# From wo on: seven tiles of 128 tokens in place of eight batches of 112, and two new orders of work

## The chip, the cores and the metric

The kernel runs on one core of a Trainium2 chip. The metric is device time in microseconds (us) of one execution, the median of several runs. Engines: TensorE (PE; its weight loads are PEld), VectorE (DVE), ScalarE (ACT), GpSimd (POOL), and SyncE (SP), which here only issues DMAs.

## The reference, cut to what matters

Eight batches of 112 tokens of width 512 go through cross-attention with 375 context rows each, and then through a mixture of eight experts of which each token takes two.

```python
h = layernorm(x)                                  # x: (8, 112, 512)
q, k_new, v_new = h @ wq.T, h @ wk.T, h @ wv.T
k, v = concat([ctx, k_new]), concat([ctx, v_new]) # 375 + 112 keys
x = x + (softmax(q @ k.T / sqrt(512)) @ v) @ wo.T
h = layernorm(x).reshape(896, 512)
probs = softmax(h @ gate_weight.T)                # 8 experts
top_v, top_i = top_k(probs, 2); top_v = top_v / top_v.sum()
for e in range(8):                                # I = 1024
    gate, up = split(h @ gate_up_proj[e].T)
    out += w[:, e] * ((silu(gate) * up) @ down_proj[e].T)
x = x + out
```

## The kernel before, in words

Each fp32 product runs as three float32r products: an operand is split into a high part (ACT copies it, functions `hi_...`) and a low part (DVE subtracts, functions `lo_...`; for the context values POOL does, `lo_v`), and PE adds high x high, high x low and low x high.

The attention goes by pairs of batches, p = 0 to 3, batch A = 2p with buffers 0 and batch B = 2p + 1 with buffers 1. `body(p)` exists once for each engine, written out by hand, and the instruction order in it is the only planner: every engine takes its list in order and waits on semaphores. On PE `body(p)` runs, for the pair: the new values (`pe_vnew`), scores (`pe_scores`), transposes of the attention weights (`pe_aT`), the attention product (`pe_attn`), the transpose of its output (`pe_oT`), and wo (`pe_wo`: twelve products of 512 columns, lines 236 to 238, into PJ). Between them it puts the projections of the next pair (`pe_proj`, quarters 0 to 3, lines 266 to 270, into the banks SC), the transposes of x2 = x + attention (`pe_x2T`, line 249), the router's logits of the pair before (`pe_logits`, line 362) and the running count of tokens for each expert (`pe_prefix`). `last_pair` is the form for p = 3, without projections.

On ACT `body(0)` takes, after the attention product of A: `do_o(A)`, `hi_c(2)` (the high part of the context keys of batch 2, tile kTh<-kTs), `hi_pj` of quarter 0, the two halves of wo's high part, `do_o(B)`, `hi_o(A)`, `hi_c(3)`, `hi_pj` of quarter 1, `hi_o(B)`. DVE follows with the low parts in the same order: `lo_c(2)`, `lo_pj`, two `lo_w(3, .)`, `center`, `lo_o(A)`, `lo_c(3)`, `lo_pj`, `lo_o(B)`, and then `x2_stats` (the residual sum and its statistics).

x lies in SBUF as `x_all`, 112 partitions by eight batches; the sum with wo's result is written over it. SP loads it in four DMAs (batches 0, 1, 2 to 3, 4 to 7), all issued in the first 15 us on one queue together with the weights and the context. Then come, in `body` order, the context keys of the next pair (each after the scores of the batch whose buffer they take), its context values, in p = 0 eight DMAs that clear the slots in DRAM, and the stores of x2.

Tokens are sent to their experts' slots by indirect DMAs from POOL (`scatter`, four for each pair). After the last pair PE takes the logits of batches 6 and 7, loads what is already in the slots of expert 0 (`pe_early`), picks the last pair's tokens by a product (`pe_pick`), and starts the experts with `pe_gu_first`. Four products of one row of zeros open accumulation groups (`pe_open`, line 428): SC[0] and SC[1] around the logits, PJ[0] and PJ[1] after the picks. `pe_idle` (line 423) are products that only keep PE busy.

The first chunk: `pe_proj_first` takes quarter 0 of the first pair as wh x xh, wl x xh for one 128-column block, then the same for the other, and at last both wh x xl; the low part of the second block comes from POOL.

Of the kernel before, what the change touches and what calls it, by code (L numbers as in the profile page):

```python
# [4 lines left out]
F32 = mybir.dt.float32  # L5
F32R = mybir.dt.float32r
# [34 lines left out]
def build_kernel(nc, x, ctxT, ctxn, w_all, gwt, units, out):  # L41
# [3 lines left out]
    with stack:  # L45
# [24 lines left out]
        tri = sb("tri", [S, S], BF16)  # L70
        ones = sb("ones", [S, S], BF16)
        iota8 = sb("iota8", [S, NE], F32)
        ebase = sb("ebase", [S, NE], F32)
        padid = sb("padid", [128, 2], F32)
        half = sb("half", [128, 8], F32)
        minus = sb("minus", [S, 2], F32)
        iotai = sb("iotai", [128, 24], I32)
        most = sb("most", [S, 2], F32)
        mosti = sb("mosti", [S, 2], I32)
        filled = sb("filled", [S, 8], I32)  # L80
# [8 lines left out]
        st2 = sb("st2", [S, 2, 6], F32)  # L89
        mv2 = sb("mv2", [S, 2, 2], F32)  # L90
        ve2 = sb("ve2", [S, 2, 1], F32)
        rs2 = sb("rs2", [S, 2, 1], F32)
        shift = sb("shift", [S, 2, 1], F32)
# [4 lines left out]
        mx8 = sb("mx8", [S, 2, 8], F32)  # L98
        ix8 = sb("ix8", [S, 2, 8], U32)
        mask = sb("mask", [S, 2, 2, 8], F32)  # L100
        mboth = sb("mboth", [S, 2, 8], BF16)
        mnew = sb("mnew", [S, 8], BF16)
        msum = sb("msum", [S, 2, 8], BF16)
        row8 = sb("row8", [S, 2, 8], F32)
        junk = sb("junk", [S, 2, 2, 8], F32)
        rowf = sb("rowf", [S, 4], F32)
        dl = sb("dl", [S, 2], F32)
        el = sb("el", [S, 2], F32)
        el1 = sb("el1", [S, 2], F32)
        idx = sb("idx", [S, 4], I32)  # L110
        gwT = sb("gwT", [128, KT, NE], F32)

        iotar = sb("iotar", [S, CAP], F32)
        away = sb("away", [S, 2], F32)
        place = sb("place", [S, 2], F32)
        iotari = at("iotari", [S, CAP], I32, top[0])

        mean = at("mean", [128, 128], F32, top[0] + size([S, CAP], F32))
        pick = [sb(f"pick{a}", [S, CAP], F32R) for a in range(2)]

        xr = sb("xr", [S, 2, 2, RW], F32)
# [8 lines left out]
        x_all = sb("x_all", [S, NB, D], F32)  # L130
# [17 lines left out]
        x2T = [at(f"x2T{a}", [128, KT, S], F32, top[0] + a * KT * S * 4) for a in range(2)]  # L148
        aTh = [sb(f"aTh{a}", [128, 4, S], F32R) for a in range(2)]
        aTl = [sb(f"aTl{a}", [128, 4, S], F32R) for a in range(2)]  # L150
        oTh = [sb(f"oTh{a}", [128, KT, S], F32R) for a in range(2)]
# [121 lines left out]
        def pe_proj_first(pe, bank):  # L273
# [5 lines left out]
            for m in range(2):  # L279
# [3 lines left out]
                for k in range(KT):  # L283
                    nc.tensor.matmul(o, wTh[0][:, k, ms], xTh[:, k, :], start=False, stop=False)
# [1328 lines left out]
```

## Time and profile before

| | us |
|---|---|
| three runs | 451.88, 452.18, 450.74 |
| median | 451.88 |
| the profiled execution | 453.74 |
| its span, first to last instruction | 452.0 |
| PE busy in it | 441.3 (98%) |
| DVE, ACT, POOL busy | 345.4, 252.0, 99.5 |

The profile is of one execution. Busy times are sums over an engine's instructions; a view by windows gives them for stretches with TensorE's granted clock. A DMA's time is from issue to landing. The attention ends at about 160 us of the span; the experts take the rest.

### The profile page before, as it was taken

To read this page: it belongs to the slowest core of one execution; us is meant where nothing else is said; L and a number is where in the kernel's file an instruction comes from. 1 tells how busy PE (TensorE), PEld (TensorE's weight loads), DVE (VectorE), ACT (ScalarE), POOL (GpSimd) and SP (SyncE) were. 2 spreads that over 40 slices of the span, in tenths; PEclk is the share of its full clock that TensorE was granted. 3 is DMA by queue.
4 is the path that set the end of the run, shared out by engine and by line. 5 is a ranking of instruction groups with operands and counts; after the bars stand their busy time and mean duration, and the time that the engine had idled before them with its cause. 6 is when DMAs were issued, how large, how long until landed. Compare 5 with 4: busy or idle time off the path is not lost.

```text
span 452.0 us, 7158 instructions
## 1 busy us (share of the span) xinstructions
PE 441.3 (98%) x2530; PEld 374.8 (83%) x2530; DVE 345.4 (76%) x647; ACT 252.0 (56%) x412; POOL 99.5 (22%) x129
## 2 busy tenths in 40 slices
PE   7999999999999999999999999999999999999993
PEld 5978888888888788888888888888888888888882
DVE  5867556656645669998988988888898898898862
ACT  4567434524625566666566666656657557566530
POOL 6061071254418343003003003003003002002111
PEclk9999999999999989999999999999999999999998
DMA  8996994434545465966856856956956956855411
GB/s 268 352 262 187 285 218 140 128 66 139 198 111 231 143 212 156 369 209 186 260 183 189 279 158 202 278 157 210 259 174 196 259 195 192 256 203 167 92 48 52
DMA packets 26943, 88.92 MB, mean 197 GB/s; under 512 B 2592, under 2 KB 8736, under 8 KB 26912
## 3 DMA queue, kind: packets, MB, share of 16 engines
q1 hardware_dynamic: 23296, 80.13, 55.0%
q0 software_dynamic: 3616, 8.41, 8.3%
q8 instruction: 16, 0.26, 0.3%
q14 instruction: 15, 0.12, 0.1%
HBM read 74.07 MB, written 14.45 MB: 196 GB/s over the span
## 4 chain that ended last, share of the span: by engine, by line
PE 93%; DVE 2%; POOL 1%; ACT 1%; DMA 1%; issue 0%; POOLq 0%; DVEq 0%
PE T L417 13%; PE PJ L417 13%; PE PJ L418 7%; PE T L418 6%; PE SC L518 3%; PE SC L519 3%; PE SC L520 3%; PE T L249 3%; PE PJ L236 3%; PE PJ L238 3%; PE PJ L237 3%; PE SC L266 3%; PE SC L270 3%; PE SC L268 3%; PE R L518 2%; PE R L519 2%
## 5 line engine op out<-in xcount | busy, mean ns | idle before, releaser
L923 DVE TENSOR_TENSOR ul<-ng,uh 128x1536 fp32r<-128x1536 f32 x64 | 112.5, 1757 | 1.0
L669 ACT ACTIVATE uh<-ng 128x1536 fp32r<-128x1536 f32 x64 | 94.7, 1480 | 0.0
L417 PE MATMUL T<-eb,uh 128*128 128x512 f32 x248 | 88.8, 397 | 0.0
L417 PE MATMUL PJ<-eb,uh 128*128 128x512 f32 x248 | 88.7, 397 | 0.0
L418 PE MATMUL PJ<-eb,ul 128*128 128x256 f32 x248 | 69.7, 281 | 0.0
L418 PE MATMUL T<-eb,ul 128*128 128x256 f32 x248 | 69.6, 281 | 0.0
L1397 POOL DMA_INDIRECT out<-ys,yidx x14 | 24.7, 1764 | 173.5 <-ACT ys L846 171.4
L417 PEld LDWEIGHTS PJ<-eb,uh 128*128 128x128 f32 x248 | 46.6, 188 | 11.3
L417 PEld LDWEIGHTS T<-eb,uh 128*128 128x128 f32 x248 | 46.6, 188 | 11.2
L418 PEld LDWEIGHTS T<-eb,ul 128*128 128x128 f32 x248 | 46.8, 189 | 1.3
L418 PEld LDWEIGHTS PJ<-eb,ul 128*128 128x128 f32 x248 | 46.7, 188 | 1.3
L1325 POOL TENSOR_TENSOR vl<-vs,vh 128x512 fp32r<-128x512 f32 (+1 forms) x24 | 30.6, 1311 | 11.7 <-DVE xr L1018 9.1
L669 ACT ACTIVATE us<-PJ 128x256 f32<-128x256 f32 x32 | 12.3, 385 | 31.4 <-PE PJ L418 31.3
L1216 DVE TENSOR_TENSOR hf<-us,hs 128x256 f32<-128x256 f32 x63 | 26.8, 425 | 2.9 <-ACT hs L864 0.8
L1218 DVE TENSOR_TENSOR hl<-hf,hh 128x256 fp32r<-128x256 f32 x64 | 27.2, 425 | 2.2
L864 ACT ACTIVATE hs<-gs 128x256 f32<-128x256 f32 x63 | 25.9, 411 | 3.6 <-DVE gs L1195 3.5
L669 ACT ACTIVATE us<-T 128x256 f32<-128x256 f32 x31 | 11.9, 385 | 28.6 <-PE T L418 28.6
L518 PE MATMUL SC<-uh,hh 128*128 128x512 f32 x64 | 26.0, 406 | 0.0
L669 ACT ACTIVATE gs<-PJ 128x256 f32<-128x256 f32 x32 | 12.3, 384 | 23.4 <-PE PJ L418 22.3
L519 PE MATMUL SC<-ul,hh 128*128 128x512 f32 x64 | 25.1, 393 | 0.0
L520 PE MATMUL SC<-uh,hl 128*128 128x512 f32 x64 | 25.1, 392 | 0.0
L1359 POOL DMA_INDIRECT slots<-xr,idx x16 | 18.3, 1141 | 20.6 <-issue 19.0
(243 smaller groups left out, 925.1 us busy)
## 6 DMA issues: line engine op xcount, KB each, us to landing
ng<-in_units SPq DMA_DIRECT2D x64, 768.0 KB, 4.4
vs<-in_ctxn SPq DMA_DIRECT2D x8, 768.0 KB, 4.9
kTs<-in_ctxT SPq DMA_DIRECT2D x8, 750.0 KB, 5.0
slots<-zero SPq DMA_DIRECT2D x8, 514.0 KB, 12.2
xe<-slots SPq DMA_DIRECT2D x8, 514.0 KB, 4.4
wTs<-in_weights SPq DMA_DIRECT2D x8, 512.0 KB, 8.3
out<-x_all SPq DMA_DIRECT2D x8, 224.0 KB, 4.6
x_all<-in_x SPq DMA_DIRECT2D x1, 896.0 KB, 19.3
```

Source lines behind the costliest of these rows:

```text
L417: nc.tensor.matmul(o[:, :].rearrange("p (h s) -> p h s", h=2), wh, both[:, k, :, :], start=k == 0, stop=False)
L418: return nc.tensor.matmul(o[:, 0:CAP], wl, both[:, k, 0, :], start=False, stop=k == KT - 1)
L518: nc.tensor.matmul(o, hh[b][:, s], wh, start=i == 0, stop=False)
L519: nc.tensor.matmul(o, hh[b][:, s], wl, start=False, stop=False)
L520: last = nc.tensor.matmul(o, hl[b][:, s], wh, start=False, stop=i == IT - 1)
L669: nc.scalar.activation(o, i, ACT.Copy).then_inc(s, 1)
L864: nc.scalar.activation(hs[b][:, :], gs[b][:, :], ACT.Silu).then_inc(silu_ok, 1)
L923: v.tensor_tensor(o, whole, hi.bitcast(F32), ALU.subtract).then_inc(s, 1)
L1216: link(v.tensor_tensor(hf[b][:, :], us[b][:, :], hs[b][:, :], ALU.mult))
L1218: v.tensor_tensor(hl[b][:, :], hf[b][:, :], hh[b][:, :].bitcast(F32), ALU.subtract)\
L1325: g_.tensor_tensor(vl[a][0:n, j, :], vs[a][0:n, j, :], vh[a][0:n, j, :].bitcast(F32), ALU.subtract).then_inc(v_lo, 1)
L1397: pool.indirect_dma_start(out[:, :], bass.IndirectOffsetOnAxis(yidx[:, e, t:t + 1], 0), ys[:, t, :], None, compute_op=ALU.add).then_inc(y_ ...
```

## The change

**Tiles.** `parts(g)` says where the tokens of batch g lie in the seven tiles of 128: 16g of them end tile g-1, the rest begin tile g. `pe_wo`, `pe_x2T`, `x2_stats`, the second norm, the logits, the top two, the prefix and the scatter now work on tile g (g = 1 to 7) at the place where batch g was, and nothing is done at the place of batch 0. So wo, the x2 transposes and the logits run seven times and not eight. `hi_o` and `lo_o` write a batch's columns into two tiles, with two instructions for batches 1 to 6. There are three buffers oTh/oTl, and `hi_o` waits for wo of three tiles before.

**x twice.** The attention reads x from `xb4` (112 partitions, four batches), the residual sum from `xt` (128 partitions, four tiles). SP loads `xb4` for batches 4 to 7 after the norms of batches 0 to 3 are done; the tiles 1 to 4 are loaded by four DMAs where batches 4 to 7 were loaded; tile 5 in p = 1, tiles 6 and 7 in p = 2.

**The last logits.** The products that open SC and PJ stand among the transposes and logits of the last tiles, and two `pe_idle` products go.

**First chunk.** The wl x xh product of the second block comes last in `pe_proj_first`; `hi_pj(0,0)` and `lo_pj(0,0)` come before the weight half (1,1); in p = 0 DVE takes `do_max(A)` before `lo_c(1,1)`.

```diff
-        x_all = sb("x_all", [S, NB, D], F32)
+        xb4 = sb("xb4", [S, 4, D], F32)
+        xt = sb("xt", [128, 4, D], F32)
...
+        def parts(g):
+            n = 16 * g
+            both = [(g - 1, 128 - n, 0, n), (g, 0, n, S - n)]
+            return [p for p in both if p[3]]
...
+            pe.wait_ge(first_hi[0], 1)
+            part(0, wTh[0], xTh)
+            pe.wait_ge(first_lo, 1)
+            part(0, wTl[0], xTh)
+            pe.wait_ge(first_hi[1], 1)
+            part(1, wTh[0], xTh)
             pe.wait_ge(x_lo, 2)
...
+            part(0, wTh[0], xTl)
+            part(1, wTh[0], xTl)
+            pe.wait_ge(first_lo, 2)
+            part(1, wTl[0], xTh, True).then_inc(pj, 1)
...
                 if p == 0:
                     pe.wait_ge(w_lo, 7)
-                pe_wo(pe, A, 0, PJ[0])
+                if p:
+                    pe_wo(pe, A, 0, PJ[0])
                 pe.wait_ge(pj_lo, 4 * p + 5)
                 pe_proj(2, SC[0])
                 pe_wo(pe, B, 1, PJ[1])
-                pe_x2T(pe, A, 0, T[0])
+                if p:
+                    pe_x2T(pe, A, 0, T[0])
...
-            pe_logit(pe, NB - 2, 0)
-            pe_x2T_half(pe, 0, T[1])
-            pe_idle(T[2], 2)
-            pe_x2T_half(pe, 1, T[0])
+            pe_logit(pe, NB - 2, 0, (0, 1))
             pe.wait_ge(expd, NB)
             pe_open(SC[0])
+            pe_x2T_half(pe, 0, T[1])
+            pe_open(GB[0][0])
+            pe_x2T_half(pe, 1, T[0])
+            pe_open(SC[1])
+            pe_logit(pe, NB - 2, 0, (2, 3))
             pe_logit_last(pe)
-            pe_open(SC[1])
+            pe_open(GB[0][1])
...
             pe_pick(pe, SC)
-            for w in range(2):
-                pe_open(GB[0][w])
             pe_gu_first(pe)
...
             hi_w(1, 0)
+            hi_pj(0, 0, SC[0])
             hi_w(1, 1)
-            hi_pj(0, 0, SC[0])
...
             def hi_o(g, a, bank):
                 act.wait_ge(o_T, g + 1)
+                if g > 2:
+                    act.wait_ge(wo_mm, g - 2)
+                for t, c, r, n in parts(g):
+                    ins = nc.scalar.activation(oTh[t % 3][:, :, c:c + n], v[:, :, r:r + n], ACT.Copy)
...
             lo_w(1, 0)
+            lo_pj(0, 0, SC[0])
             lo_w(1, 1)
-            lo_pj(0, 0, SC[0])
...
                 if p == 0:
                     norm_x(p + 1)
+                do_max(A, 0)
+                if p == 0:
                     lo_c(1, 1)
-                do_max(A, 0)
...
-            sp.dma_start(x_all[:, 4:NB, :], xv[:, 4:NB, :]).then_inc(x_in[3], 16)
+            for g in range(1, 5):
+                load_xt(g)
+            sp.wait_ge(x_norm, 4)
+            sp.dma_start(xb4[:, :, :], xv[:, 4:NB, :]).then_inc(x_in[3], 16)
```

## Rows read from the trace of the kernel before

**Rows 1.** The page: the chain that ended last, shares of the span by engine.

```profile
PE 93%; DVE 2%; POOL 1%; ACT 1%; DMA 1%; issue 0%; POOLq 0%; DVEq 0%
```

**Rows 2.** Waits of PEld, first 180 us: total, times, longest in us.

```profile
PEld PJ L236 <- DVE oTl L923: 0.9, 2, 0.6
```

**Rows 3.** Timeline, first chunk: start, us, engine, line, operation, tile, idle before.

```profile
10.42 0.71 PE L287 MATMUL SC<-xTh,wTl 128*128 128x224 f32 x4 [0.16 <-POOL wTl L1319]
11.86 0.61 PE L266 MATMUL SC<-xTh,wTh 128*128 128x224 f32 x4
...
14.81 0.67 PE L266 MATMUL SC<-xTh,wTh 128*128 128x224 f32 x4
...
25.64 1.72 DVE L923 TENSOR_TENSOR kTl<-kTs,kTh 128x1500 fp32r<-128x1500 f32 x1
...
27.27 0.66 DVE L985 TENSOR_REDUCE mx<-SC 112x1 f32<-112x487 f32 x1
...
28.96 0.60 PE L249 MATMUL T<-ident,ex 112*128 112x112 f32 x4 [0.37 <-ACT ex L711]
```

**Rows 4.** Timeline of the first pair, 37 to 55 us.

```profile
37.22 1.45 ACT L669 ACTIVATE kTh<-kTs 128x1500 fp32r<-128x1500 f32 x1
...
38.70 1.72 DVE L923 TENSOR_TENSOR kTl<-kTs,kTh 128x1500 fp32r<-128x1500 f32 x1 [1.30 <-ACT kTh L669]
...
45.76 0.46 PE L236 MATMUL PJ<-wTh,oTh 128*112 128x512 f32 x1
...
46.76 0.62 DVE L923 TENSOR_TENSOR oTl<-T,oTh 128x448 fp32r<-128x448 f32 x1
...
48.60 0.60 PE L266 MATMUL SC<-xTh,wTh 128*128 128x224 f32 x4
...
51.27 0.39 PE L236 MATMUL PJ<-wTh,oTh 128*112 128x512 f32 x1
...
54.05 0.55 PE L249 MATMUL T<-ident,x_all 112*128 112x112 f32 x4
54.36 0.69 PE L266 MATMUL SC<-xTh,wTh 128*128 128x224 f32 x4
```

**Rows 5.** Chain in order of time: the logits of one pair.

```profile
103.53 1.48 PE R L362 x16
```

**Rows 6.** DMAs: the queue's timeline; issues with KB and us to landing.

```profile
14.23 0.44 SPq L1458 DMA_DIRECT2D x_all<-in_x  x1
25.84 6.96 SPq L1437 DMA_DIRECT2D kTs<-in_ctxT  x2
...
x_all<-in_x SPq DMA_DIRECT2D x2, 224.0 KB, 2.9
x_all<-in_x SPq DMA_DIRECT2D x1, 896.0 KB, 19.3
kTs<-in_ctxT SPq DMA_DIRECT2D x1, 750.0 KB, 9.4
```

**Rows 7.** Windows: us, busy of each engine, granted clock, DMA share, GB/s.

```profile
21.00:25.00 4.00, 4.00 (x20) 3.08 (x19) 3.67 (x9) 1.79 (x2) 0.70 (x1) 1.00 1.02 397
26.00:30.00 4.00, 3.63 (x19) 2.57 (x18) 2.65 (x4) 2.18 (x5) 3.33 (x3) 1.00 1.06 227
...
161.00:162.00 1.00, 1.00 (x9) 0.84 (x9) 0.89 (x5) 0.04 (x1) 0.70 (x1) 1.00 0.98 322
...
163.00:164.00 1.00, 1.00 (x7) 0.94 (x7) 0.18 (x2) 0.91 (x2) 0.00 (x0) 0.50 0.86 209
```

**Rows 8.** Chain and timeline from 162 to 169 us.

```profile
162.16 2.01 PE SC L436 x8
...
164.76 1.42 PE SC L436 x8
...
168.06 0.53 PE PJ L428 x2
...
168.26 1.29 DVE L923 TENSOR_TENSOR eb<-SC,eb 128x512 fp32r<-128x512 f32 x2 [0.81 <-ACT eb L669]
```

**Rows 9.** Groups of ACT by shape: busy us, mean ns, idle before.

```profile
L669 ACT ACTIVATE oTh<-T 128x448 fp32r<-128x448 f32 x8 | 4.3, 541 | 2.8 <-PE T L249 2.8
L669 ACT ACTIVATE us<-T 128x256 f32<-128x256 f32 x1 | 0.4, 385 | 0.3 <-PE T L418 0.3
```

More of the change, by code:

```diff
@@ L97, in build_kernel @@
         rinv = sb("rinv", [S, 2, 1], F32)
[L98 to L110, printed above, removed]
-        gwT = sb("gwT", [128, KT, NE], F32)
[L113 to L121, printed above, removed]
+        mx8 = sb("mx8", [128, 2, 8], F32)
+        ix8 = sb("ix8", [128, 2, 8], U32)
+        mask = sb("mask", [128, 2, 2, 8], F32)
+        mboth = sb("mboth", [128, 2, 8], BF16)
+        mnew = sb("mnew", [128, 8], BF16)
+        msum = sb("msum", [128, 2, 8], BF16)
+        row8 = sb("row8", [128, 2, 8], F32)
+        junk = sb("junk", [128, 2, 2, 8], F32)
+        rowf = sb("rowf", [128, 4], F32)
+        dl = sb("dl", [128, 2], F32)
+        el = sb("el", [128, 2], F32)
+        el1 = sb("el1", [128, 2], F32)
+        idx = sb("idx", [128, 4], I32)
+        gwT = sb("gwT", [128, KT, NE], F32)
+        iotar = sb("iotar", [128, CAP], F32)
+        away = sb("away", [128, 2], F32)
+        place = sb("place", [128, 2], F32)
+        iotari = at("iotari", [128, CAP], I32, top[0])
+        mean = at("mean", [128, 128], F32, top[0] + size([128, CAP], F32))
+        pick = [sb(f"pick{a}", [128, CAP], F32R) for a in range(2)]
+        xr = sb("xr", [128, 2, 2, RW], F32)
         o_w = top[0]
@@ L375, in pe_logit_last @@
                     pe.wait_ge(half_Tok, k // 2 + 1)
-                last = nc.tensor.matmul(R[0:S, 8:16], x2T[1][:, k, :], gwT[:, k, :], start=k == 0, stop=k == KT - 1)
+                last = nc.tensor.matmul(R[:, 8:16], x2T[1][:, k, :], gwT[:, k, :], start=k == 0, stop=k == KT - 1)
             last.then_inc(logits, 1)
         def pe_logits(pe, p):
-            pe_logit(pe, 2 * p, 0)
-            pe_logit(pe, 2 * p + 1, 1)
+            for a in halves(p):
+                pe_logit(pe, 2 * p + a, a)
         def pe_prefix(pe, p):
@@ L472, in pe_gu_first @@
                     pe.wait_ge(summed, 1)
-                    nc.tensor.matmul(T[2][0:S, 0:8], ones[:, :], mnew[:, :], start=True, stop=True).then_inc(total, 1)
+                    nc.tensor.matmul(T[2][:, 0:8], ones[:, :], mnew[:, :], start=True, stop=True).then_inc(total, 1)
                 pe.wait_ge(e_lo, h + 1)
@@ L776, in body @@
                 do_exp(A, 0)
-                if p:
+                if p > 1:
                     second_row(A - 2, 0)
```

277 lines of the change are left out of this document (151 added, 126 removed).

## The prediction

> **What bounds the kernel now.** I read the chain first, then the waits of TensorE, then timelines of the three stretches that the change touches. The reader is to see in the chain that PE holds 93% of it [rows 1], and in the waits that in the whole attention PE's weight loads waited for DVE's oTl only 0.9 us, in two places [rows 2]. Between about 29 and 151 us the chain names nothing but PE instructions, one behind the other. So the attention is a list of PE instructions, and what leaves that list is time saved, as long as no other engine or transfer becomes later than PE. Before 29 us PE has gaps, and behind 159 us a short chain through several engines leads into the experts, which the change leaves alone. The question is therefore: how much leaves PE's list, and what is then late.
>
> **Work that goes.** In the first pair PE no longer does wo for batch 0. Its products start at 45.76 and the next piece starts at 48.60: 2.84 us [rows 4]. The x2 transposes of that batch go as well, from 54.05 to 54.36: 0.31 us [rows 4]. In the second pair half of the logits go, 16 products in 1.48 us being two batches: 0.74 us [rows 5]. The seven tiles that stay have the same twelve products of 512 moving columns; 128 columns of weights in place of 112 load beside the product before. Sum: 3.89 us. POOL has two indirect DMAs fewer, DVE one residual sum with its statistics, all beside PE, worth nothing.
>
> **First chunk.** Three edits, each of which removes a gap of PE.
> - The second block's low part makes PE start at 10.42 what it could have started at about 10.09 (the four products before take 0.44 us), and proj quarter 1 starts at 11.86 [rows 3]. With that product last, quarter 1 starts at about 11.42: 0.44 us.
> - Quarter 2 starts at 14.81, 2.95 us behind quarter 1; a quarter takes 2.67 us, so 0.28 us is the wait for SC[0], which `lo_pj(0,0)` frees. With it ahead of the weight half it is done at about 13.3. Together 0.72 us.
> - The transposes of batch 0's attention weights start at 28.96, after the chain lo_c (25.64, 1.72 us), maximum (27.27), exponential [rows 3]. With the maximum ahead of `lo_c(1,1)` the exponential ends near 26.9 and PE is the later one, at 28.43 - 0.72 = 27.7. `lo_c(1,1)` then ends at about 27.8, and scores of batch 1 need it at 28.1; it just fits. Together 1.25 us, bounded by 0.7 (if that fit fails) and 1.3.
>
> **What is late next: the first pair's wo.** PE would reach wo of tile 1 at 51.27 - 2.84 - 1.25 = 47.18 [rows 4]. It needs `lo_o(B)`. DVE's list from the start of `lo_c(2)` at 38.70 to the end of `lo_o(B)` at 46.76 + 0.62 takes 8.68 us [rows 4]; part of that was waiting for PE's quarter 1, now earlier, so I take 8.1 to 8.7, and 0.15 for the split copy. `lo_c(2)` follows `hi_c(2)`, 1.48 us later, and that needs batch 2's context keys. They are issued at 25.84 and land 9.4 us later, at 35.2; ACT took them at 37.22, so nobody waited [rows 4, 6]. Now the queue holds more ahead of them: tiles 1 to 4 of x (1.05 MB) where batches 4 to 7 stood, and then batches 4 to 7 as well. The load of batches 4 to 7 as it was was issued at 14.23 and landed at 33.5 [rows 6]; it and the keys now shift by the time of the four tile loads. Such 128-partition traffic ran at 397 GB/s from 21 to 25 us, while the window in which the 112-partition x passed shows 227 GB/s [rows 7]. That is 2.6 us by the faster row and 4.6 by the slower; I take 2.75, being 128-partition loads of whole rows. The keys land at 38.0, `lo_c(2)` starts at 39.5, `lo_o(B)` ends between 47.7 and 48.3, and PE waits 0.5 to 1.1 us at wo; I take 0.7. With the keys at 35.2 + 4.6 = 39.8 it would be 2.5. Below nothing it can't go. The wait for the last of wo's low parts, ahead of quarter 2, lies about four us before that end on DVE and is met.
>
> The issues themselves: SP now waits for the norms of batches 0 to 3 before it issues the second x load, and the next pair's keys stand behind it; the norms end near 25.1 and the keys are issued near 26 as before. Loads of tile 5 (second pair) and 6 and 7 (third) stand behind waits for the x2 stores two pairs earlier; what is queued behind these waits are the pair's own stores, with no reader before the end.
>
> Here the traces show DMAs of 224 KB that landed after 2.9 us each though issued half a microsecond apart [rows 6]. The Trainium skill (SBUF — State Buffer, "The DMA setup-cost knee") counts roughly 2 us for every DMA and advises one large transfer over several, which speaks against four tile loads. An estimate by that page, with the four paid in turn, puts 8 us on the queue in addition. By the row they overlap, and it adds nothing. The result that it would give is the rival on the other side below.
>
> **Splitting hi_o and lo_o.** A copy of 448 elements takes 541 ns and one of 256 takes 385 [rows 9]: 0.81 ns an element, 0.18 fixed. The second instruction costs about 0.1 to 0.2 us on each of ACT and DVE. In pairs 0 to 2 a projection quarter (2.67 us) lies between transpose and wo and hides it. In the last pair nothing does: PE already waits there, 0.9 us in two places [rows 2]. Only batch 6 is split, batch 7 goes to one tile: 0.2 us, bounded by 0 and 0.4.
>
> **The tail.** The two products that open PJ, 0.53 us at 168.06, leave the path; but the products behind them need DVE's first low part, begun at 168.26, so some 0.2 us of it is gained [rows 8]. Among the logits two more products of this kind stand, 0.2 us each, while two idle products go: about 0.1 us later. Net gain 0.1, bounded by -0.3 and +0.4. In this stretch PE's clock fell from 1.00 to 0.50 of 2.4 GHz, that is to 1.2 GHz, though the profile has PE busy ahead of it [rows 7]: the first 8 records of L436 took 2.01 us, the second 1.42, both in part at half clock [rows 8]. The new order puts 512-column products where small ones stood. I take the dip as it is; if it goes, it gives 1.2 us; if it lengthens by one us, 0.5 is lost.
>
> **Sum.** 3.89 + 1.25 - 0.7 - 0.2 + 0.1 = 4.3 us off. For the profiled execution: 453.74 (span 452.0 and 1.74 around it) - 4.3 = 449.4. It was 1.9 above the median of the runs shown; for the median 451.88 - 4.3 = 447.6 us.
>
> **The rivals.**
> - Slow tile loads, 0.2: tiles move like the 112-partition x. PE waits 2.5 us in the first pair and not 0.7: 449.4. For it: they have the same 2 KB pieces. Against it: keys and weights beside them ran at 397 GB/s.
> - The clock stays up in the tail, 0.15: 446.4. For it: more columns between 159 and 162 us. Against it: a row of zeros is a light product, and idle products stood there too.
> - The first chunk gives little, 0.08: `lo_c(1,1)` or a weight load is late and only about 0.3 remains: 448.6.
> - Loads in turn, 0.03, the other side: each tile load takes the 2.9 us of rows 6 alone, 11.6 us on the queue. Keys at 46.8, wo at 56.6 in place of 47.2, a wait of 9.4 us: net 451.88 + 9.4 - 5.0 = 456.3. It decides from where the keys land later than about 42.5, when the wait eats the 5.0 us of the other terms. Against it: the queue was full all through the first 30 us and moved 397 GB/s with eight DMAs in it.
>
> **How the numbers follow.** The forecast has 0.54. Its own terms give 446.6 to 448.4. The clock rival reaches to 445.4 with no wait at wo, slow loads to 450 with the worst of the tail. Range 445.4 to 450.0. About 0.3%, 1.4 us, is what a measurement of this kernel can tell from no change. Faster by more needs a median below 450.5: all of the forecast, the clock and the chunk cases and nine tenths of slow loads: 0.94. Within 0.3%: 0.03. Slower: 0.03.
>
> **What would show it.** In the new profile: wo lines L236 to L238 with 84 products and not 96; the wait of PEld on oTl in the first pair near 47 to 48 us, at 0.5 to 1.1; ACT's kTh<-kTs for batch 2 beginning at 38 after a DMA wait; the first aT transposes at 27.7; vnew of the second pair 4.3 us earlier. It would be wrong if PE waits over 1.5 us for oTl, if new PE gaps appear in pairs 1 and 2, or if the low clock near 162 us grows.

## The result, and the profile after

The changed kernel takes 451.21 us (median of 22 runs, 448.43 to 453.17), the kernel before 452.31 us on the same chip (22 runs, 450.47 to 454.45). The ratio is 0.9966, with a 95% interval of 0.9952 to 0.9981: by the ratio 1.5 us less, between 0.9 and 2.2 (the two medians lie 1.1 apart). The prediction was 4.3 us less. The sign was right, the size nearly three times too large, and 451.21 lies outside the range of 445.4 to 450.0.

The profiled execution of the changed kernel took 450.01 us, its span is 448.2. Taken alone, the two profiles would nearly have confirmed me: 452.0 - 448.2 = 3.8 us. But the profile of before was 1.4 us above its median, the one of after is 1.2 us under it. The two sections of the page that answer to the table of before and to [rows 1], busy time and the chain:

```profile
PE 437.3 (98%) x2504; PEld 372.0 (83%) x2504; DVE 343.9 (77%) x645; ACT 251.5 (56%) x416; POOL 101.8 (23%) x130
...
PE 89%; DMA 3%; DVE 2%; issue 2%; POOL 2%; ACT 1%; SPq 0%; POOLq 0%; DVEq 0%; ACTq 0%
```

PE has 4.0 us less work. In the chain PE fell from 93% [rows 1] to 89%, and DMA rose from 1% to 3%: more of the path is waiting for transfers. That is the first sign of what went wrong.

The attention came out near the forecast. In the first pair, timeline of 37 to 53 us (start, length, engine, line, tile, in brackets the idle time before), against [rows 4]:

```profile
37.51 1.46 ACT L699 ACTIVATE kTh<-kTs 128x1500 fp32r<-128x1500 f32 x1 [1.28 <-DMA kTs<-in_ctxT]
39.00 1.72 DVE L959 TENSOR_TENSOR kTl<-kTs,kTh 128x1500 fp32r<-128x1500 f32 x1 [2.69 <-ACT kTh L699]
...
46.23 0.67 DVE L1036 TENSOR_TENSOR oTl<-T,oTh 128x64 fp32r<-128x64 f32 x2
47.42 0.40 PE L259 MATMUL PJ<-wTh,oTh 128*128 128x512 f32 x1
```

ACT takes the keys of batch 2 at 37.51, after a wait for the DMA (I had said 38.0), and wo of tile 1 starts at 47.42 (I had said 47.2 plus a wait). What PE waits for oTl in all is in the list of PE's waits of the first 180 us (total, times, longest), against [rows 2]. Both waits are in the last pair, at 148.31 and 151.64; in the first pair, where I had priced 0.7 us, there is none:

```profile
PEld PJ L259 <- DVE oTl L1036: 1.0, 2, 0.7
```

In the last pair the last of wo's high products starts at 154.27, and it was at 158.43: 4.16 us earlier, where my terms for this part add up to 4.24. That agreement is partly luck, as the last part shows; from there on the forecast breaks openly. Four stages of the span, from the timelines (start of that product; first product into T of unit 1 of the experts; last product; end of span):

| us | last wo | to the experts | experts | to the end | span |
|---|---|---|---|---|---|
| before | 158.43 | 13.12 | 272.37 | 8.1 | 452.0 |
| after | 154.27 | 12.20 | 273.43 | 8.3 | 448.2 |

In the tail between wo and the experts the clock did not fall in this execution, where it had fallen for 3.4 us in the profile of before, and the tail got 0.9 us shorter; the experts, which the change does not touch, got 1.1 us longer. What made them longer is on SP's queue. Timeline of SP, 163 to 185 us, and ACT's copy of the same weights, timeline of 171 to 190 us:

```profile
166.61 0.33 SPq L1555 DMA_DIRECT2D ng<-in_units  x1
176.58 0.89 SPq L1571 DMA_DIRECT2D xe<-slots  x2
178.53 4.61 SPq L1555 DMA_DIRECT2D ng<-in_units  x4
```

```profile
179.37 1.47 ACT L699 ACTIVATE uh<-ng 128x1536 fp32r<-128x1536 f32 x1
185.49 1.49 ACT L699 ACTIVATE uh<-ng 128x1536 fp32r<-128x1536 f32 x1 [2.06 <-DMA ng<-in_units]
```

SP waits until the last pair's scatters have landed before it loads the slots (xe), and the weights of the next units (ng) stand behind that wait. The wait ended 10.1 us after the experts began (176.58 against 166.47); in the kernel before it was 7.8 (179.40 against 171.55). PE had become earlier, and the scatters had not become earlier by as much. The next weights so left 2.3 us later in terms of PE, ACT waited 2.06 us, and ahead of 197.89 PE stood still for 0.70 us.

### The profile page after: what moved, and what is told of

It reads as the page before. It is cut to its first block, busy times and chain, and to the rows that moved or that the text cites. A ratio compares the mean times of both kernels' runs of the same rounds, so it can differ in the third digit from the quotient of the medians.

```text
span 448.2 us, 7127 instructions
## 1 busy us (share of the span) xinstructions
PE 437.3 (98%) x2504; PEld 372.0 (83%) x2504; DVE 343.9 (77%) x645; ACT 251.5 (56%) x416; POOL 101.8 (23%) x130
## 4 chain that ended last, share of the span: by engine, by line
PE 89%; DMA 3%; DVE 2%; issue 2%; POOL 2%; ACT 1%; SPq 0%; POOLq 0%; DVEq 0%; ACTq 0%
PE PJ L444 12%; PE T L444 11%; PE PJ L445 6%; PE T L445 6%; PE T L272 3%; PE PJ L259 3%; PE PJ L261 3%; PE PJ L260 3%; PE SC L289 3%; PE SC L291 3%; PE SC L293 3%; PE SC L545 3%; PE SC L546 3%; PE SC L547 3%; PE R L545 2%
## 5 line engine op out<-in xcount | busy, mean ns | idle before, releaser
L1378 POOL TENSOR_TENSOR vl<-vs,vh 128x512 fp32r<-128x512 f32 (+1 forms) x24 | 31.6, 1353 | 10.8 <-DVE xr L1060 8.8
L1412 POOL DMA_INDIRECT slots<-xr,idx x14 | 20.4, 1460 | 14.9 <-issue 13.5
```

The source lines that it names most:

```text
L1378: g_.tensor_tensor(vl[a][0:n, j, :], vs[a][0:n, j, :], vh[a][0:n, j, :].bitcast(F32), ALU.subtract).then_inc(v_lo, 1)
```

## The experiments

Times are medians; all of a row's runs share one chip with runs of the kernel before, and the ratio is against those. The chips differ from group to group: e1 to e5 ran on one, e9 to e12 on a second, e13 to e16 on a third, e17 to e20 on a fourth, and the changed kernel beside the 452.31 above. Across groups the ratios are the fairer comparison. The third column is the mean over the runs of the granted clock of the whole span. It counts the half clock behind PE's last product as well, when PE has nothing left to do: in the profiles this is some 2 to 6 us. 3.4 us of half clock lower the mean by 0.0038, so one run's mean says little, but one below 0.9895 (9.5 us of half clock) points to a fall before the end.

| kernel | us | mean clock | ratio, 95% interval |
|---|---|---|---|
| before (35, 35, 23, 22 runs on the four chips) | 452.12, 452.17, 452.37, 452.18 | 0.995 to 0.996 | |
| changed kernel | 451.21 | 0.9905 | 0.9966 [0.9952, 0.9981] |
| e3: before + tail order | 453.35 | 0.992 | 1.0034 [1.0014, 1.0054] |
| e5: before + first chunk | 451.32 | 0.995 | 0.9984 [0.9965, 1.0003] |
| e12: before + tiles alone | 449.64 | 0.996 | 0.9961 [0.9936, 0.9987] |
| e4: tiles and first chunk | 449.70 | 0.995 | 0.9952 [0.9933, 0.9970] |
| e1: changed + two units first | 452.12 | 0.991 | 1.0008 [0.9994, 1.0022] |
| e9: e4 + two units first | 452.07 | 0.993 | 0.9991 [0.9967, 1.0015] |
| e10: e4 + late tile loads | 449.12 | 0.994 | 0.9931 [0.9907, 0.9955] |
| e11: e10 + two units first | 450.70 | 0.994 | 0.9963 [0.9939, 0.9987] |
| e15: e10 + one unit first | 447.72 | 0.996 | 0.9907 [0.9873, 0.9941] |
| e13: changed + late tile loads | 449.80 | 0.992 | 0.9954 [0.9930, 0.9977] |
| e14: e13 + idle products | 450.55 | 0.991 | 0.9952 [0.9926, 0.9978] |
| e16: e13 + clears of 128 rows | 448.37 | 0.997 | 0.9897 [0.9867, 0.9927] |
| e19: changed + clears of 128 rows | 449.95 | 0.996 | 0.9954 [0.9937, 0.9972] |
| e20: before + clears of 128 rows | 452.09 | 0.995 | 0.9989 [0.9976, 1.0002] |
| e18: e15 + clears of 128 rows | 448.19 | 0.995 | 0.9914 [0.9893, 0.9936] |
| e17: changed + all three mends | 446.96 | 0.996 | 0.9891 [0.9867, 0.9915] |

One profiled execution of a kernel, in stages (us; half clock between wo and the experts; from the start of the last wo to the experts; ACT's wait for their weights; the experts; from the start of the last product to the end of the span):

| | half clock | to the experts | ACT's wait | experts | to the end |
|---|---|---|---|---|---|
| before | 3.4 | 13.12 | 0 | 272.37 | 8.1 |
| e5 | 0 | 11.51 | 0 | 272.28 | 8.6 |
| e20 | 0 | 11.18 | 0.53 | 272.41 | 8.6 |
| changed | 0 | 12.20 | 2.06 | 273.43 | 8.3 |
| e4 | 0 | 11.65 | 1.84 | 273.25 | 8.4 |
| e10 | 0 | 11.65 | 1.29 | 272.70 | 8.6 |
| e15 | 0 | 11.65 | 0 | 272.48 | 6.9 |
| e1 | 6.8 | 15.30 | 0 | 272.30 | 8.4 |
| e13 | 3.4 | 13.80 | 0 | 272.20 | 8.4 |
| e16 | 0 | 11.49 | 1.51 | 272.87 | 8.3 |
| e17 | 0 | 11.48 | 0 | 272.52 | 6.9 |
| e18 | 0 | 11.21 | 0 | 272.19 | 8.2 |

The last column says how far a single execution may be trusted. In e12, e15 and e17 the span ends 6.9 us behind the start of the last product, in the fifteen other profiles 8.1 to 8.8, with the same work in it. This 1.4 us is as large as the steps below; why the end is short or long, no run here shows.

### The parts of the change

**The new order of the last logits, alone** (e3) and **taken away** (e4). The edit of e4, and in reverse of e3, in `_(pe)`:

```
-            pe_logit(pe, NB - 2, 0, (0, 1))
-            pe.wait_ge(expd, NB)
-            pe_open(SC[0])
-            pe_x2T_half(pe, 0, T[1])
-            pe_open(GB[0][0])
-            pe_x2T_half(pe, 1, T[0])
-            pe_open(SC[1])
-            pe_logit(pe, NB - 2, 0, (2, 3))
+            pe_logit(pe, NB - 2, 0)
+            pe_x2T_half(pe, 0, T[1])
+            pe_idle(T[2], 2)
+            pe_x2T_half(pe, 1, T[0])
+            pe.wait_ge(expd, NB)
+            pe_open(SC[0])
             pe_logit_last(pe)
-            pe_open(GB[0][1])
+            pe_open(SC[1])
...
+            for w in range(2):
+                pe_open(GB[0][w])
             pe_gu_first(pe)
```

> The kernel before with the new order of the last logits alone. Clock theory: the dip to half clock at 162 to 166 us goes and with it about 1.2 us, together with the products that open PJ: 1.0 to 1.4 us faster, mean clock 0.996 and up. Queue theory: the same at the start of the experts, but the scatters' landing moves less, so 0.3 to 1.0 us of it is left. If the dip only came by chance in the profiled execution: within 0.3 us of the kernel before.

> The changed kernel with the old order of the last logits and the old place of the products that open PJ. Clock theory: 1.2 us slower than the changed kernel, with the half clock back near 158 to 162 us in the profile. Queue theory: the experts start 1.3 us later but their stall shrinks by as much, so within 0.5 us of the changed kernel.

Measured: put into the kernel before, the new order costs (453.35 against 452.12, ratio wholly above 1); taken out of the changed kernel, it gives 1.5 us (449.70 against 451.21). By the ratios the second is 0.6 us, and the two intervals overlap; e3 alone is clear of noise (1.5 us, between 0.6 and 2.4).

The clock is one part of it. Of the 22 runs of the changed kernel 11 had a mean clock under 0.9895, of the 12 of e4 none, of 35 runs of before one. The median of those 11 is 451.97, of the other 11 it is 450.39. In the profile of e3 half clock lasted 6.8 us, in that of before 3.4 us.

The order itself is the other part. Where no half clock falls into the tail, it takes 11.65 us from the last wo to the experts in e4, e10, e12 and e15 (old order) and 12.20 in the changed kernel; with wide clears (below) it takes 11.21 in e18 (old) and 11.49 in e16, e17 and e19 (new). So the new order is 0.3 to 0.55 us longer where I had it 0.1 shorter, and "I take the dip as it is" did not hold either.

**The first chunk alone** (e5: before with the new order of the products, of `lo_pj(0, 0)` and of the maximum).

```
+            part(0, wTh[0], xTl)
+            part(1, wTh[0], xTl)
+            pe.wait_ge(first_lo, 2)
+            part(1, wTl[0], xTh, True).then_inc(pj, 1)
...
+            lo_pj(0, 0, SC[0])
             lo_w(1, 1)
-            lo_pj(0, 0, SC[0])
```

> The kernel before with the new order of the first chunk alone. Everything behind it moves together, the scatters and the loads behind them too, so both theories say 1.0 to 1.25 us faster than before (about 451.2 against 452.3), and the aT transposes of batch 0 start at 27.7 to 27.9 in the profile. If the first chunk's gain is lost later: within 0.3 us of the kernel before.

Measured: 0.8 us less in the median (ratio 0.9984, interval up to 1.0003), and in its profile the first transposes of attention weights start at 27.83 where they had started at 28.96 [rows 3], the last wo at 157.25 and not at 158.43. But the profiles of e3 and e20, whose code is that of before up to there, have 28.62 and 28.60, and the last wo at 158.09 and 158.05. Against these the edit gives 0.8 us, against the profile of before 1.1 to 1.2, and whatever it gives at the transposes reaches the last wo. The median says 0.8 too.

**The tiles alone** (e12: the changed kernel with the old first chunk and the old tail order, both edits as above in reverse).

> Only the seven tiles of 128: the first chunk and the last logits in the order of before. By the prediction's terms the tiles save 3.9 us less 0.9 of waits, 3.0 us: 449.1. By the theory of three losses: the same 3.0 at the last wo, less 1.0 in the expert stage and 0.5 to 2 in the last pair, so 0 to 1.5 us under before: 450.6 to 452. Rival 'tiles give nothing': 452.1. The old tail's half clock should be as long as in before (0 or 3.4 us).

Measured: 449.64, ratio 0.9961, so 1.8 us less with an interval from 0.6 to 2.9. My terms gave 3.0. With the first chunk on top (e4) it is 449.70, ratio 0.9952. The tiles carry most of the gain, and the median lies short of their terms, though the interval nearly reaches them.

### A scatter that lands late

In the last pair, DVE's norm of the second tile overwrites the rows that the second pair's scatter reads. Timelines of 112 to 144 us; first the changed kernel:

```profile
113.49 0.84 SPq L1515 DMA_DIRECT2D xt<-in_x  x2
114.04 1.10 POOL L1412 DMA_INDIRECT slots<-xr,idx  x1 [4.39 <-issue]
...
120.04 5.78 SPq L1527 DMA_DIRECT2D out<-xt  x2
...
130.74 0.55 DVE L1060 TENSOR_SCALAR xr<-xt,mv,rs 128x512 f32<-128x512 f32 x1 [1.29 <-DMA slots<-xr,idx]
131.37 7.51 POOL L1378 TENSOR_TENSOR vl<-vs,vh 128x512 fp32r<-128x512 f32 x6 [4.15 <-DVE xr L1060]
```

Then e4, which has the same code up to the tail:

```profile
133.17 0.55 DVE L1060 TENSOR_SCALAR xr<-xt,mv,rs 128x512 f32<-128x512 f32 x1 [3.66 <-DMA slots<-xr,idx]
133.80 7.49 POOL L1378 TENSOR_TENSOR vl<-vs,vh 128x512 fp32r<-128x512 f32 x6 [6.51 <-DVE xr L1060]
...
136.66 0.92 DVE L1080 TENSOR_TENSOR mask<-iota,ix 128x32 f32<-128x32 f32 x1
137.62 1.19 DVE L1084 TENSOR_TENSOR mboth<-mask 128x16 bf16<-128x16 f32 x1
138.85 1.22 DVE L1091 TENSOR_TENSOR mnew<-mboth 128x8 bf16<-128x8 bf16 x1
140.10 1.21 DVE L1093 TENSOR_TENSOR msum<-msum,mnew 128x8 bf16<-128x8 bf16 x1
...
143.66 0.57 PE L272 MATMUL T<-ident,ex 112*128 112x112 f32 x4 [1.67 <-ACT ex L741]
```

The reader is to follow five steps. SP issues the loads of tiles 6 and 7 half a microsecond ahead of POOL's four scatters, where the kernel before had no loads of x any more. The scatters land 10.6 us after their issue in the changed kernel, 13.7 in e4 and 6.4 in the kernel before (medians). DVE waits for them, 1.29 and 3.66 us. POOL's `lo_v` starts behind that norm, and beside it DVE's smallest operations take 1.2 us each: `mnew` and `msum`, 8 elements a row, took 0.16 in the changed kernel, where POOL's pieces were ending as they began (138.82; 131.37 + 7.51 = 138.88), and 1.22 and 1.21 here. That delays the maximum and the exponential of the last batch, and PE stands still for 1.67 us ahead of 143.66. In e4 the last wo came at 156.40, and so 2.1 of the 4.2 us were gone; in e19, with a wait of 3.38 us, it came at 157.99 and only 0.4 was left. The Trainium skill (SBUF — State Buffer, "Who interferes with whom") has it that a DVE instruction with two inputs in SBUF contends with a GpSimd instruction that reads SBUF. The rows agree: `mnew` and `msum` have two such inputs, and they went from 0.16 to 1.2 us beside `vl<-vs,vh`; `mboth`, whose two inputs are halves of `mask`, took 1.19 us in this pair in the changed kernel too, and 0.17 to 0.18 in the other pairs, where POOL's pieces had ended.

**Late tile loads** (e10 on e4; e13 on the changed kernel). The loads of tiles 6 and 7 go behind the stores of tiles 4 and 5:

```
-                    for g in ((5,) if p == 1 else (6, 7)):
-                        load_xt(g)
+                    if p == 1:
+                        load_xt(5)
                     store_x2(A)
                 store_x2(B)
+                if p == 2:
+                    load_xt(6)
+                    load_xt(7)
```

> The changed kernel with the old order of the last logits, and with the loads of x tiles 6 and 7 issued behind the stores of tiles 4 and 5, so that they do not share the queues with the second scatter. Theory 'late scatter': DVE's wait for that scatter ahead of the norm of tile 5 falls from 3.66 us (0.97 to 3.7 in the three profiles with early loads) to under 0.5, lo_v starts before 132 us, and PE's stall at the last aT goes; median 448.7 to 449.3, up to 2 us under the profile of the old tail order. Rival 'the 256 KB stores of x2 or POOL's four descriptors make it late, not the loads': the scatter still lands after more than 10 us, the wait stays, 449.7. Rival 'tiles 6 and 7 now land late': DVE waits for them ahead of the last residual sums, which the old cover of 20 us excludes by a wide margin.

> The changed kernel with one edit: the loads of x tiles 6 and 7 go out behind the stores of tiles 4 and 5. With the old tail order this edit gave 0.6 us (449.70 to 449.12). Theory 'two separate losses': the new tail order costs the same 1.5 us as it did beside early loads, so 450.6 us (0.6 under the changed kernel's 451.2), with most executions at a mean clock under 0.993. Rival 'the stall in the last pair is what lets the clock fall in the tail': with the stall gone the dips go too, 449.1 and a mean clock of 0.994 or more.

The same rows in e10:

```profile
118.43 0.96 POOL L1412 DMA_INDIRECT slots<-xr,idx  x1 [0.30 <-issue]
120.08 5.71 SPq L1527 DMA_DIRECT2D out<-xt  x2
125.83 0.93 SPq L1515 DMA_DIRECT2D xt<-in_x  x2
128.88 0.99 DVE L1060 TENSOR_SCALAR xr<-xt,mv,rs 128x512 f32<-128x512 f32 x2
129.96 7.50 POOL L1378 TENSOR_TENSOR vl<-vs,vh 128x512 fp32r<-128x512 f32 x6 [2.77 <-DVE xr L1060]
```

The two norms run as one piece, nothing waits for the DMA, `lo_v` starts at 129.96, and the last wo at 153.96. The scatters landed after 8.8 us: still more than 6.4, but early enough. All profiles agree: in the six of kernels with early tile loads (changed, e1, e4, e9, e12, e19) these scatters landed after 10.4 to 13.7 us and DVE waited 0.97 to 3.66, in the eight with late ones after 8.3 to 9.6, with a wait of 0 to 0.65. In the median the edit gave 0.6 us beside the old tail order and 1.4 beside the new one (449.80 against 451.21); by the ratios it is 0.9 and 0.5. No single interval excludes zero for either step; it is the profiles that show the mechanism. The rival that the stall alone lets the clock fall in the tail is out: e13 has no stall, its mean clock is 0.992, and its profile has 3.4 us of half clock in the tail.

### Weights behind the scatter wait

**Two units first** (e1 on the changed kernel, e9 on e4, e11 on e10). The slot loads with their wait go behind two more weight loads; the first round of the experts is written out for it.

```
+            def slots_in():
+                sp.wait_ge(x2_out, 16 * (NB - 1) + 16 * 2)
+                for a in range(2):
+                    sp.wait_ge(scattered[a], sent(a, PAIRS))
...
                 for u in range(UB):
+                    if early and u == 2:
+                        early()
...
+            experts(0, 0, 2, 2 * ER, early=slots_in)
-            with sp.Fori(0, NE // 2 - 1) as j:
+            with sp.Fori(1, NE // 2 - 1) as j:
```

> The changed kernel, with two more loads of expert weights issued ahead of the wait for the last scatters and the two slot loads. Queue theory: in the changed kernel the attention ends 4.2 us earlier and the experts begin 5.5 us earlier, but the loads behind that wait come only 2.8 us earlier, ACT waits 2.1 us for weights and the expert stage loses 1.7 us; here ACT's wait for weights is gone and the time falls by 1.0 to 2.0 us against the changed kernel, to about 449.7 us. Clock theory: the expected gain is lost to a lower granted clock in most executions (0.986 to 0.993 against 0.996 in the profiled one); the order of the loads is then no matter and the time stays within 0.5 us of 451.2.

> The changed kernel with the old order of the last logits, and with the loads of the second expert's first two units issued ahead of the wait for the last scatters. Theory 'three losses' (the new tail order costs 1.5 us through the clock; a weight load queued behind the scatter wait costs 1.0 us in the expert stage; a late scatter costs 0.5 to 2 us in the last pair): the expert stage falls from 273.3 to 272.3 us, ACT's wait for ng goes, the median is 448.7 us, 1.0 under the run with the old tail order alone (449.70). Rival 'the wait is slack': the wait of ACT goes but PE finds another one, the median stays at 449.7.

> All three mends together: old order of the last logits, units ahead of the scatter wait, late loads of tiles 6 and 7. If the losses are separate and add up: 1.0 plus 0.4 to 1.0 under 449.7, that is 448.0 (447.6 to 448.4), near the 447.6 that was predicted for the change. If the clock takes up what is freed: 449 or above with a mean clock under 0.995.

All three missed. In the profile of e1 ACT's wait is gone (experts 272.30 us, from 273.43), but there half clock in the tail had let the experts begin late, and e13, without this edit, has 272.20 after such a tail: e1 doesn't show what the edit does. Its median was 0.9 above the changed kernel's, and e9 and e11 were 2.4 and 1.6 us slower than the kernels they were made from. Timeline of SP in e9, PE's next transposes there, and PE's windows (us, busy, clock, DMA share, GB/s):

```profile
167.27 8.61 SPq L1555 DMA_DIRECT2D ng<-in_units  x3
179.23 1.49 SPq L1571 DMA_DIRECT2D xe<-slots  x2
```

```profile
184.66 0.65 PE L272 MATMUL R<-ident,xe 128*128 128x128 f32 x4 [1.85 <-DMA xe<-slots]
```

```profile
182.00:184.00 2.00, 0.81 (x5) 1.00 0.96 329
184.00:186.00 2.00, 1.34 (x8) 1.00 0.97 355
186.00:188.00 2.00, 2.00 (x8) 0.52 0.95 393
188.00:190.00 2.00, 2.00 (x9) 0.63 0.23 91
```

The last scatter was issued at 169.65, and the slots could be loaded only at 179.23: 9.6 us, where the changed kernel needed 7.3 (169.25 to 176.58). The two extra weight loads of 768 KB were in the queues beside the scatter, and the very transfer came late that SP's wait is for. PE had no slack for it, stood still for 1.85 us, and then ran 3.4 us at half clock; e11's profile has the same. It looks like the mechanism of the last pair, now set off by my own mend. In e1's profile PE hardly waits for the slots (0.2 us), so this does not explain why e1 is slow; its tail has 6.8 us of half clock.

**One unit first** (e15 on e10: `u == 1` in place of `u == 2`).

> Old tail order and late tile loads, and one unit load (not two) goes out ahead of the wait for the last scatters. With two, the loads of the slots came 2.9 us later, PE waited 4.1 us for them at 181 us and then ran 3.4 us at half clock (450.70 against 449.12). Theory 'a unit load in the queues slows the scatter in front of the slots': one load costs about half of that delay, 1.2 us, which PE has no slack for, but ACT's wait for ng of 1.3 us goes: 449.1 within 0.7 either way, and the expert stage between 272.3 and 274. If the loss of two units had to do with iteration 0 being written out rather than with the order, this is as slow as with two, 450.7.

Measured: 447.72, 1.4 us under e10. SP issues the slot loads at 176.17, 10.6 us after the experts began (165.54), ACT waits for no weights, and the experts take 272.48 us. The first round is written out here too, so that was not what made the others slow; the order was. How much the edit is worth is open: the two ratios give 1.1 us with overlapping intervals, on two chips and with six runs of e15. Of the 2.0 us between the two profiles' spans only 0.2 lies in the experts, and 1.7 behind the last product, which the edit does not touch.

What the wait for weights costs can be read across the profiles of the table above: with no wait of ACT the experts take 272.2 to 272.5 us, with 0.53 us 272.41, with 1.29 272.70, with 1.51 272.87, with 1.84 273.25, with 2.06 273.43. So it is between nothing and 1.1 us. And it does not add to half clock in the tail: after a slow tail (e1, e13) PE comes to the experts late, and nothing waits.

### What lets the clock fall in the tail

Windows of PE from 156 us in e1, which has the new tail order:

```profile
156.00:158.00 2.00, 2.00 (x13) 1.00 0.66 244
158.00:160.00 2.00, 2.00 (x11) 0.67 0.89 283
160.00:162.00 2.00, 2.00 (x15) 0.50 0.97 292
162.00:164.00 2.00, 2.00 (x12) 0.50 1.00 402
164.00:166.00 2.00, 2.00 (x13) 0.62 0.19 77
```

PE is busy 2.00 of every 2.00 us and its clock still halves. The chain of e1 in order of time (start, length, tile, line) shows what PE does then: transposes (L272), eight-column logits (L388, L403) and the clearing products (L455), which multiply one row of zeros by one row of zeros:

```profile
155.63 0.32 PE SC L455
155.95 0.37 PE T L272 x2
156.32 0.32 PE PJ L455
156.64 0.37 PE T L272 x2
157.01 0.32 PE SC L455
157.32 0.54 PE R L388 x4
157.87 0.89 PE R L403 x8
158.76 0.54 PE PJ L455
```

The last clear takes 0.54 us where the ones before took 0.32: there the clock has fallen. The Trainium skill (TensorE: Matmul & The Clock Gate, Part 1) describes a gate that goes by how busy PE has been. The profile has PE busy all through these rows and the clock falls, so its busy column doesn't tell when that happens. Two edits change the products of this stretch.

**Idle products back** (e14 on e13).

```
             pe_open(GB[0][0])
+            pe_idle(T[2], 2)
             pe_x2T_half(pe, 1, T[0])
```

> As the run with late tile loads and the new tail order, and the two idle products that the change removed are back between the two halves of the last transposes (0.2 to 0.3 us of products). Theory 'the light stretch is longer in the new order because the heavy 256-column products are gone': the clock holds more often, 449.3 to 449.8. Rival 'the order of the opens matters, not these': no change or 0.2 us slower, 450.6 to 450.8.

Measured: 450.55 and a mean clock of 0.991: 0.75 above e13's median, at the same ratio. The two idle products changed nothing that these runs can tell.

**Clearing products of 128 rows** (e16 on e13, e19 on the changed kernel, e20 on before). The columns stay as they are. The expectation of e16 has it that the time does so too; that is answered below:

```
-            nc.tensor.matmul(bank[:, :], zero[0:1, 0:64].bitcast(BF16), zero[0:1, 0:256].bitcast(BF16),
+            nc.tensor.matmul(bank[:, :], zero[:, 0:64].bitcast(BF16), zero[:, 0:256].bitcast(BF16),
```

> As the run with late tile loads and the new tail order, and the products of zeros that clear the banks use all 128 rows instead of one (same columns, so the same time each; PE gets no further waits). Theory 'one-row products count as an almost idle TensorE': with them wider the clock falls in fewer executions, 449.3 to 449.8, mean clock 0.994 or more. Rival 'their zeros count as nothing in any width, or they play no part': same as with one row, 450.6.

> The changed kernel with one edit: the clearing products read 128 rows of zeros instead of one. Theory 'the rows decide the clock in the tail': mean clock from 0.990 to 0.995 or more, the median from 451.2 to 449.0 to 449.5 (the 1.5 to 2 us that the longer half clock cost), with the scatter wait and the weights wait unchanged. Rival 'wide opens helped only because the late tile loads had taken the stall before them': 450.5 to 451.2 with the clock as low as ever.

> The kernel before with the same edit of the clearing products. Theory 'the rows decide': the dip of 3.4 us at 162 us goes in nearly all executions, 450.8 to 451.5 (1 to 1.5 us under before), mean clock over 0.997. Rival 'before's dip has another cause (few products beside the last residual sum)': no change, 452.2.

Measured: e16 is 1.4 us under e13, at a mean clock of 0.9967 against 0.9918, and in e19 the clock rises from 0.9905 to 0.9955. None of e19's 11 runs is under 0.993, where half of the changed kernel's are under 0.9895. So the edit of the clearing products keeps the clock up in the new tail order. Windows of e17, which has them wide, from 154 us:

```profile
154.00:156.00 2.00, 1.99 (x12) 1.00 0.81 234
156.00:158.00 2.00, 2.00 (x18) 1.00 0.74 274
158.00:160.00 2.00, 2.00 (x21) 1.00 0.78 267
160.00:162.00 2.00, 2.00 (x19) 1.00 0.97 302
```

But it does more than that. The chain of e17 in order of time, one clear and the transposes behind it, against 156.32 and 156.64 of e1, both at full clock:

```profile
156.28 0.21 PE PJ L455
156.50 0.22 PE T L272 x2
```

A clear takes 0.21 us and not 0.32, and the two transposes behind it 0.22 and not 0.37. At full clock the tail takes 11.49 us in e16, where the changed kernel's took 12.20: 0.7 us, about half of the edit's 1.4, needs no clock. The two effects come with one edit, so these runs don't show whether the clock stays up for the rows that the products use or for the shorter stretch.

In time, e19's gain is 1.3 us by medians taken on two chips, but only 0.5 by the ratios, whose intervals overlap. Its profile is that of its slowest run, and shows what the edit leaves untouched, PE's windows in the last pair:

```profile
142.00:144.00 2.00, 0.32 (x4) 1.00 0.00 0
144.00:146.00 2.00, 2.00 (x8) 0.55 0.01 2
146.00:148.00 2.00, 2.00 (x7) 0.60 0.68 261
```

The scatter's stall, 1.85 us ahead of 143.68, is itself followed by 3.4 us at half clock. The two cost 3.4 us: from the first transposes of attention weights to the last wo e19 takes 129.89 us, e16 and e17 126.4 and 126.5. It is not always so: in e4 PE stood still for 1.67 us at the same place and the clock stayed at 1.00. In the kernel before, wide clears gave 0.1 us by the median (452.09) and 0.5 by the ratio, with an interval that holds zero: the third expectation missed. Its tail at full clock is 0.3 us shorter (11.18 in e20, 11.51 in e5). Its mean clock did not rise, so something other than the clears decides in that order; what, these runs don't show.

### The mends together

e17 has late tile loads, one unit first and wide clears in the changed kernel; e18 has the same with the old tail order.

> The changed kernel (its own tail order) with three mends: late tile loads, one unit load ahead of the scatter wait, clearing products of 128 rows. If they are separate: 448.4 (late loads and wide opens) less 0.7 to 1.4 for the unit load: 447.0 to 447.7. If the unit load's gain in the last call was chance: 448.4.

> The same three mends with the old order of the last logits. Without wide opens it took 447.7. Theory 'with the clock held the old order is the shorter by 0.6 us': 0.3 to 0.7 under the same kernel with the new order, 446.8 to 447.4. Rival 'the idle products it keeps cost what its order gives': equal.

Measured: e17 took 446.96 us, ratio 0.9891 [0.9867, 0.9915]: 4.9 us under before with an interval of 3.8 to 6.0, and under the interval of the changed kernel. It is the fastest of all, and its slowest run (448.52) is about as fast as the fastest of the changed kernel (448.43). e18 is 1.2 us slower, not faster as I had expected. The tail of its profile is the shorter one as expected (11.2 us against 11.5), and its mean clock over the runs is lower, 0.9947 against 0.9963; in which stage the runs lose it, one profile doesn't show. With six runs of each the two intervals overlap.

## Why the prediction was wrong

**What leaves PE's list: too large by 0.4 us, and hidden by luck.** From the first transposes of attention weights to the last wo, before takes 129.47 us and e10, which has no stall there, 126.12: 3.35 us less, with 0.1 us of added waits in it. So about 3.45 left the list, and I had 3.89. wo of batch 0 is right: the first pair goes on from these transposes to wo of tile 1 in 19.5 us, as worked out. What I put at nothing is that tiles of 128 make the small products dearer: 16 logits take 1.69 us in the chain and not 1.48, four transposes of x2 0.44 and not 0.39. The sum at the last wo (4.16 against 4.24) came out because waits that I had priced at 0.9 us were 0.1.

**First chunk: right in what it removes.** 1.25 forecast; 0.8 to 1.2 at the last wo of e5, according to which profile of the old order it is held against; transposes at 27.93 in the changed kernel against a forecast of 27.7. The rival "gives little" (0.3) is out by the profiles.

**The wait in the first pair: did not come.** Keys were taken at 37.51, forecast 38.0, and `lo_o(B)` ended at 46.90, ahead of PE. PE's whole wait for oTl in 180 us is 1.0 us, all in the last pair, against 0.9 before [rows 2]. I had priced 0.7 and 0.2 more, and 0.1 came. Slow tile loads (0.2) and loads in turn (0.03) did not come: the four loads overlapped, as [rows 6] had suggested.

**Splitting hi_o and lo_o: fair.** In the groups by shape ACT's piece of 128x64 takes 218 ns and the one of 128x384 takes 496, together 0.17 us over the 541 of one piece [rows 9].

**The tail: the first failed step.** The term was +0.1 us, bounded by -0.3 and +0.4, and "I take the dip as it is". At full clock the new order takes 12.20 us where the old one takes 11.65: -0.55, beyond the bound. The chain shows it: each clear among the transposes costs 0.32 us, and the two transposes behind it take 0.37 us and not 0.22. The dip did not stay as it was either: half of the changed kernel's runs are under a mean clock of 0.9895, and their median is 1.6 us above that of the others. In the kernel before, the new order alone costs 1.5 us (e3). Part of this stood in [rows 7]: the clock had fallen to 0.50 with PE busy in every window, so putting other products into that stretch was no neutral act.

**"All beside PE, worth nothing": the second.** I counted the scatters that went and not those that stayed. I asked of the tile loads only whether their readers would be late, and wrote of what is queued behind their waits that it had no reader before the end. But a transfer that shares the queues with them, the second pair's scatter, had a reader: DVE's norm. At the last wo that costs 0.2 us in the changed kernel's profile (126.34 against 126.12), 2.35 in e4's and, with the half clock behind it, 3.4 to 3.8 in e19's. In the medians it is 0.5 to 1.4 (e10, e13).

**"The experts, which the change leaves alone": the third.** They had a wait in SP's order that PE's gain of 4 us uncovered: 1.1 us in the changed kernel's profile, less in the others. In the three profiles with a slow tail behind the tiles (e1, e13, e14) no such wait is there, so this step and the first don't add up.

How far these rows go, as an estimate from the profiles at full clock on both sides: the last wo comes 3.8 to 4.2 us earlier (against e3 and e20, and against before), the tail is 0.7 longer (12.20 against 11.51 in e5), the experts 1.1. That leaves 2.0 to 2.4 us of the forecast's 4.3, inside the measured interval of 0.9 to 2.2 or just above it. The runs with half clock pull the median down further: without them it would be 450.39 and not 451.21.

What the mends gave, by the medians and by the ratios: late tile loads 1.4 and 0.5 us (e13 against the changed kernel; 0.6 and 0.9 in e10 against e4), wide clears 1.4 and 2.6 (e16 against e13), one unit first 1.4 and 1.1 (e15 against e10). All three together took the ratio from 0.9966 to 0.9891, 3.4 us of 452, and 4.2 by the medians. That is more than was missing, so some of it was paid by the kernel before as well; how much, these runs don't show. The interval of each single step is about as large as the step; only the sum is sure.

Still open: through what the wide clears keep the clock up in the new order while they don't in the order of before, why the end of the span is 1.4 us shorter in some executions, and whether e18 is slower than e17 by more than chance.

## What to carry to other kernels

When PE gets earlier by four microseconds, list every semaphore wait whose source does not get earlier with it, and what stands behind that wait in its queue; such waits turn up in stages that the edit never touches. In these profiles a load issued beside an indirect scatter delayed the scatter, and the waiter of the scatter paid, so ask of each new transfer what else is in flight, not only who reads it. Check a sum term by term and not by its total: here two terms were wrong by 0.4 and 0.8 us and cancelled. And compare medians before profiles, and profiles stage by stage: two single executions showed 3.8 us where 44 runs showed 1.5.

## What was not expected of the hardware

- The second pair's indirect scatters landed after 6.4 us in the kernel before (112 rows, no loads of x beside them), 8.3 to 9.6 in the eight profiles with late tile loads and 10.4 to 13.7 in the six with two 256 KB loads just ahead of them. From the issue of the last pair's last scatter to the loads of the slots it was 9.6 us with two more 768 KB loads ahead of the wait (e9) and 7.3 without (changed kernel).
- DVE operations of 8 elements a row took 0.16 us alone and 1.2 us beside POOL's subtraction of 128x512.
- The granted clock fell to 0.50 with PE busy 2.00 of 2.00 us. Widening products of zeros from 1 to 128 rows raised the mean clock from 0.9918 to 0.9967 (e13, e16); the clears then took 0.21 us and not 0.32 at full clock, and the transposes behind them 0.22 and not 0.37.
- A stall of PE of about 1.8 us was followed by 3.4 us at half clock in two places (143.7 us in e19, 184.7 us in e9), one of 1.67 us in e4 was not.
